# Lead of the query-row scores over the transposed scores in four-head attention tiles: two tiles before, one and a half after

## What is computed

```python
x = L0(x, ctx)      # causal self attention, cross attention, feed-forward; 16 heads of 16
x = L1(x, ctx)      # masked self and cross attention, 8 experts of which 2 per token; 16 heads of 16
x = L2(x, ctx)      # self and cross attention with masks and biases, feed-forward; 16 heads of 16
x = L3(x, ctx)      # causal cross attention, layer norm; 8 heads of 32

def attention(q, k, v, mask):          # per head
    s = q @ k.T * scale                # 512 x 512
    s = where(mask, -big, s)
    return softmax(s, axis=-1) @ v
```

## Time and profile before

| what | value |
| --- | --- |
| median of three executions | 2725.34 us |
| the profiled execution | 2719.28 us |
| its span | 2717.3 us |
| PE busy | 2500.1 us, 92% of the span |
| DVE busy | 1783.6 us, 66% |
| ACT busy | 1381.5 us, 51% |
| POOL busy | 739.8 us, 27% |
| mean granted clock of PE | 0.956 of 2.4 GHz |

### The profile page before, as it was taken

How to read it: one execution, slowest core, us unless ns; L and a number is a source line. 1 busy time by engine, 2 the same in 40 slices (tenths; PEclk the granted TensorE clock), 3 DMA queues, 4 the chain that set the end, 5 groups by cost and what they waited for, 6 DMA issues and landing times. The chain is left out here.

```text
span 2717.3 us, 44289 instructions
## 1 busy us (share of the span) xinstructions
PE 2500.1 (92%) x16014; PEld 1373.0 (51%) x16014; DVE 1783.6 (66%) x4364; ACT 1381.5 (51%) x1921; POOL 739.8 (27%) x867
## 2 busy tenths in 40 slices
PE   6999999988999999997999997799999999797896
PEld 3544433333444444443999997334434444385553
DVE  3566777777677777774457774577777777455554
ACT  1544455544555555555357875255555555452332
POOL 2243335433321110201016564102222112223012
PEclk7999999989999999998899999699999999998998
DMA  6222222122133223220127785422322322001331
GB/s 177 53 50 71 58 61 65 37 54 61 43 96 94 70 75 92 78 53 25 40 86 217 221 221 130 115 71 78 108 61 73 91 73 60 9 1 42 83 85 41
DMA packets 102212, 218.54 MB, mean 80 GB/s; under 512 B 19116, under 2 KB 35372, under 8 KB 100716
## 3 DMA queue, kind: packets, MB, share of 16 engines
q1 hardware_dynamic: 93164, 203.66, 27.5%
q0 software_dynamic: 8832, 12.06, 2.4%
HBM read 100.34 MB, written 12.58 MB: 42 GB/s over the span
## 5 line engine op out<-in xcount | busy, mean ns | idle before, releaser
L1120 ACT ACTIVATE probT_a<-scores 128x1024 f32<-128x1024 f32 (+3 forms) x832 | 779.0, 947 | 712.5 <-PE scores L951 420.6
L1228 DVE CUSTOM_DVE_ANT_0 ring<-ring,maskb_a 128x512 f32<-128x512 f32 x1024 | 686.3, 716 | 172.9 <-PE ring L969 163.6
L969 PE MATMUL ring<-stacks_a 64*128 64x512 f32 (+7 forms) x1664 | 468.2, 461 | 53.3 <-DVE negm_a L1226 17.3
L990 PE MATMUL outputs<-probT_a,V_a 128*32 128x512 f32 (+6 forms) x3328 | 443.9, 576 | 12.5 <-ACT oT_a L1129 8.5
L1226 DVE TENSOR_REDUCE negm_a<-ring 128x1 f32<-128x512 f32 (+3 forms) x640 | 332.1, 563 | 139.7 <-PE ring L975 105.4
L930 PE MATMUL scores<-stacks_a 64*128 64x512 f32 (+7 forms) x1664 | 399.7, 449 | 2.4 <-DMA stacks_a<-narrow_a 2.4
L969 PEld LDWEIGHTS ring<-stacks_a 64*128 64x128 f32 (+1 forms) x1664 | 211.7, 190 | 376.0 <-issue 140.2
L930 PEld LDWEIGHTS scores<-stacks_a 64*128 64x128 f32 (+1 forms) x1664 | 170.7, 187 | 249.6 <-issue 151.9
L889 POOL TENSOR_SCALAR maskb_a<-ints_a 128x1024 bf16<-128x1024 int32 x31 | 112.8, 3639 | 423.5 <-DMA ints_a<-in_mask 353.4
L899 POOL TENSOR_TENSOR ve<-mv,epsilon 128x1 f32<-128x1 f32 x96 | 18.2, 190 | 725.0 <-DVE mv L1195 725.0
L951 PE MATMUL scores<-maskT_a,identb 64*64 64x512 bf16 x1024 | 211.0, 402 | 0.0
(11 more groups left out here) (240 smaller groups left out, 3741.0 us busy)
## 6 DMA issues: line engine op xcount, KB each, us to landing
stacks_a<-parts_a SPq DMA_DIRECT2D x672, 128.0 KB
raw<-in_moew SPq DMA_DIRECT2D x92, 512.0 KB, 3.9
ints_a<-in_mask SPq DMA_DIRECT2D x31, 512.0 KB, 3.7
swapped_a<-maskT_a SPq DMA_DIRECT2D x32, 256.0 KB, 3.7
wt<-in_w SPq DMA_DIRECT2D x7, 1024.0 KB, 4.9
kvT_a<-in_ctxT SPq DMA_DIRECT2D x12, 512.0 KB, 3.4
wrow<-in_row SPq DMA_DIRECT2D x7, 512.0 KB, 5.9
stacks_a<-narrow_a SPq DMA_DIRECT2D x224, 8.0 KB
```

The lines of the kernel that those rows point to most:

```text
L969: last = pe.matmul(bank("S", j, n, e)[:, 0:w], Q[rows, g, qt * P:(qt + 1) * P], K[rows, g, 0:w], start=True, stop=not a.causal)
L990: last = pe.matmul(OB[x * slot:(x + 1) * slot, q0:S], V[:, m % 2, kb, c:c + slot], probT[:, kb % 2, x, q0:S], start=(kb == 0), stop=(kb == ...
L1120: act.activation(probT[:, kb % 2, 2 * p:2 * p + 2, q0:S], scores_bank(j, n)[:, :, q0:S], ACT.Exp, bias=0.0, scale=-1.0).then_inc(c_exp.sem, 1)
L1228: least = dve.tensor_tensor_reduce(sc, sc, maskb[:, m % 2, qt, :], 1.0, BIG * 2, ALU.add, ALU.min, out)
```

## The change

S of half h of the list no longer belongs to the tile two on. With 8 halves, the first four halves of tile j carry S of halves 4 to 7 of tile j+1, and the last four carry S of halves 0 to 3 of tile j+2. With 4 halves it is 2 and 2. S of tile j+1 thus ends with half 3 of tile j (half 1 in a6) and no longer with half 7 of tile j-1. split moves from half 0 to half 3 (1 in a6), m and mrows from half 2 to half 5 (from 1 to 2 in a6). Nothing else moves; no instruction is added or removed.

```diff
@@ timetable
     for u in range(QT):
         out += [(u * h + 1 + late, "oT", 0, u - 1), (u * h, "stack", 0, u + 3),
-                (u * h, "split", 0, u + 1), (u * h + step, "m", 0, u + 1),
-                (u * h + step, "mrows", 0, u + 1)]
+                (u * h + h // 2 - 1, "split", 0, u + 1), (u * h + h // 2 - 1 + step, "m", 0, u + 1),
+                (u * h + h // 2 - 1 + step, "mrows", 0, u + 1)]
@@ schedule
         for h in range(halves):
+            ahead, at = divmod(halves // 2 * 3 + h, halves)
             kinds = (("ST", "S", "exp") if not reorder else ("ST", "exp", "S") if h % couples else ("S", "ST", "exp"))
             for kind in kinds:
-                if kind == "S" and there(j + 2):
-                    yield (kind, j + 2, h)
+                if kind == "S" and there(j + ahead):
+                    yield (kind, j + ahead, at)
```

## The result

The changed kernel takes 2741.95 us (median of 8 runs, 2735.74 to 2750.48); the kernel before, on the same chip, 2724.89 (8 runs, 2718.28 to 2728.38). The ratio is 1.0065, 95% interval 1.0049 to 1.0081: **slower by some 17 us**, where 17 us faster were forecast. The profiled execution took 2742.99 us with a span of 2741.0; the one before had a span of 2717.3. The two profiles are thus 23.7 us apart, since the profiled execution of before lies 6 us under its median.

A forecast was written before the change was run, and what follows sets the result against it. The prediction took the masked stages, 64 of 112 tiles, as bound by PE's own work. Its terms, 4.9 + 6.4 + 1.1 + 4 + 2 - 1.4 = 17.0 us less, gave 2708 us, range 2694 to 2722.

The forecast's parts named there:

- the drain: End of a block, without S: shorter halves before mrows is needed, nothing to 1 us once per block; taken as nothing.
- a step that I had down at 1.4: In a6, m moving from half 1 to 2 loses 3.6 us cover, gives back half of 4.5: net -1.4.
- The two terms that were priced: In a6: lost cover for PE's waits before PV, 3.6 us; half of m's 4.5 us wait for DVE's norms regained.
- mrows comes late: Rival, chance 0.08: in a0 and a6 ST waits for mrows; at 1 us a tile 31 us more, 2739.
- First block: Start of a0: first V into PE's wait, m earlier, m to ST shorter; ST 8.2 us earlier, net gain 4.9.
- the third term: Start of a0: m to ST falls from 8.27 us to 4.5, with two halves of S left: 3.8 less.
- Second and third block: Starts of a4 and a6: second gains net 6.4 us (8.5 less 2.1 for returning S), third 1.1 (2.8 less 1.7).
- Masks: In a4 and a5, S comes four halves later against the mask, DVE's waits go: 4 us, between 2.5 and 5.3.
- Layer norm stretches: In a0, S's wide extremes no longer coincide with DVE's norms: 2 us gained, between 0 and 4.5.
- The clock comes back: Rival, chance 0.20: in a0 and a1 half the slow-clock loss behind the norms' waits ends; 15 us more gained, 2693.
- V stays where it counts: Rival, chance 0.18: at the starts V waits, or the second V costs what the first saves; 9 us go, 2717.
- It washes out: Rival, chance 0.09: the starts gain, a6 and the norms give it back; 2724.

The follow-up runs named there:

- m_only: Kernel before with only split, m and mrows moved to the later halves, S left where it was: 2758.76 us, ratio 1.0114.
- after_oT3: Changed kernel with ACT's copy oT one half earlier except in u = 1: 2718.66 us, ratio 0.9974.
- v_ahead: Kernel before with only the first V of each block's first unit put ahead of its first S: 2722.82 us, ratio 0.9993.
- one_half: Kernel before with S one half later in the list, split and m where they were: 2723.50 us, ratio 0.9992.
- after_oT: Changed kernel with ACT's copy oT one half earlier in every tile: 2746.15 us, ratio 1.0066.
- after_m4: Changed kernel with m and mrows one half earlier (half 4) where a tile has eight halves: 2744.27 us, ratio 1.0070.
- after_fill: Changed kernel with the projections of half 4 put into half 2 (half 1 in the third block), the place m left: 2745.15 us, ratio 1.0072.
- before_oT3: Kernel before with ACT's copy oT one half earlier except in u = 1: 2703.89 us, ratio 0.9919.

## Why the prediction was wrong

**The step that failed** is the first one: "the masked stages, 64 of 112 tiles, are bound by PE's own work. The change adds and removes no instruction there, so their pace stays". That PE is busy 75.84 of 76.50 us says that nothing is waited for in the order of before. It does not say by how little. m was costed at the cover it gives in a6 only, where the trace already showed a wait ahead of the V product; in the masked stages hardly any of that wait was in the trace because m stood in front of it. The rule that I had written for a6 (m's 0.6 us are part of the cover of oT) holds in the masked tiles with u = 1 and u = 3 too, at 0.50 us in the tile shown, and the new place had a price of its own, 0.37. Per unit of a2 and a3 that is 0.88 + 0.88 - 0.24 = 1.5 us (u = 2 takes 0.24 less), in a4 and a5 1.1 to 1.3; the tiles u = 1 to 3 of the 16 masked units took 20 us more, the masks' gain left out. Most of the rest was lost in a0, where m's move was named but not priced, and at the end of a6, where the drain was put at nothing. m_only shows the sum: 32 us for a step that I had down at 1.4, with the masks' gain already taken off.

**a6.** The two terms that were priced came out near: from a6's first exp on, PE's waits before the V products, for oT and for the exponentials, grew by 3.8 us (8.7 to 12.5; 3.6 forecast), and m's fell from 4.5 to 2.3 (half of it was forecast). But a6 took 12.6 us more, not 1.4, and 9.4 of these are at its end, where two tiles took 4.3 and 5.2 us more: the drain, which the prediction put at nothing. m_only has 4.2 and 4.1 there, so this too comes mostly with the move of split, m and mrows. after_oT3 gives 10.2 us of a6 back with the copy alone, but the kernel before gains 7.3 there by the same copy. Timeline, PE, kernel after:

```profile
2694.75 0.60 PE L1015 MATMUL ring<-identf,mx_a 128*32 128x128 f32 x4 [1.87 <-DVE mx_a L1238]
...
2700.55 1.22 PE L931 MATMUL scores<-stacks_a 128*128 128x512 f32 x2 [2.05 <-DMA stacks_a<-narrow_a]
```

m waits for split, the next ST for mrows, and then the granted clock is down for 17.1 us. Windows, kernel after and kernel before:

```profile
2696.40:2713.50 17.10, 13.57 (x54) 7.06 (x54) 3.41 (x8) 4.01 (x7) 0.73 (x1) 0.50 0.10 33
```

```profile
2680.00:2690.00 10.00, 8.96 (x59) 4.44 (x58) 2.34 (x6) 4.60 (x9) 1.70 (x3) 1.00 0.17 55
```

That is the rival "mrows comes late", with 11.1 us in 11 waits (2.4 in one before), 7.1 of them in eight of a6's tiles, where it had 31, and nearly none in a0's tiles (0.4). Which of the waits brings the clock down there was not tried.

**First block.** Timeline, PE, kernel after:

```profile
38.45 0.47 PE L970 MATMUL ring<-stacks_a 64*128 64x128 f32 x2 [7.46 <-DMA stacks_a<-swapped_a]
...
39.05 3.73 PE L1054 MATMUL ring<-wt,xT_a 128*128 128x256 f32 x8
...
55.04 1.06 PE L1015 MATMUL ring<-identf,mx_a 128*32 128x128 f32 x4
...
59.16 0.79 PE L931 MATMUL scores<-stacks_a 64*128 64x512 f32 x2 [0.90 <-DMA stacks_a<-narrow_a]
```

The first V (it stands in the second tile before the block, not the third) did go into the wait (11.16 us in the earlier trace rows, 7.46 now), and from m to ST it is 4.12 us, against 4.5 forecast. But m comes at 55.04, as before at 55.07: ST is 4.2 us earlier, not 8.2, and first S to ST takes 20.7 us, not 16.1. What failed is the step that V's 3.3 us and the half of S ahead of m (1.1) bring m forward: the work that was left ahead of m took as long as all of it had. Windows of that stretch, kernel after and kernel before:

```profile
43.50:53.00 9.50, 9.35 (x26) 4.45 (x25) 5.89 (x14) 0.00 (x0) 0.00 (x0) 0.50 0.28 64
```

```profile
43.90:53.00 9.10, 7.94 (x37) 4.40 (x36) 6.02 (x12) 1.20 (x2) 0.00 (x0) 1.00 0.33 77
```

Before, S ran at 2.4 GHz there; I had read the clock from 53 us on only. Now all of it and the second V (3.73 us, 1.95 before) run at 1.2 GHz. Going by the row was right for the third term: m to ST is 4.15 us shorter, 3.8 were forecast. The Trainium skill ("TensorE: Matmul & The Clock Gate", What's actually happening) has sustained work lift the clock. The trace after disagrees as that of before did: PE busy 9.35 of 9.5 us stayed at the low level.

**Second and third block.** The starts got shorter, and by more than forecast: first S to ST 18.8 us (1744.71 to 1763.51; 21.2 forecast), m to ST 4.14; the seam is 9.0 us shorter, where 8.5 was the sum before S's return. The halves of S that return cost less than I took: 0.9 us at the end of each of the two blocks (last tiles of a3 and a5 against m_only), not 2.1 to 3.3. Third block: 12.6 us from first S to ST (13.0 forecast), the seam 4.7 shorter (2.8). Which of the terms was larger than forecast is open; v_ahead has V's alone at 1.3 and 0.5 us.

**Masks.** DVE's wait for maskb is gone, and the size was near: tiles 74, 78 and 82, counted from 0 through all stages, fell by 2.46, 1.71 and 1.14 us, of which some 0.23 each is what every tile with u = 2 lost; 4.6 are left (4 forecast). The reason given, that S comes four halves later, is not the only one: m_only leaves S where it was, and they fell there by 2.45, 1.72 and 1.16. In the kernel before POOL waited for the second mask load (timeline, POOL):

```profile
1944.66 3.63 POOL L889 TENSOR_SCALAR maskb_a<-ints_a 128x1024 bf16<-128x1024 int32 x1 [5.86 <-DMA ints_a<-in_mask]
```

In m_only the same instruction:

```profile
1970.92 3.63 POOL L889 TENSOR_SCALAR maskb_a<-ints_a 128x1024 bf16<-128x1024 int32 x1 [3.51 <-DMA ints_a<-in_mask]
```

In three units of before POOL waited that long (5.9, 5.1 and 4.6 us); in m_only and in the changed kernel it waited 3.5 to 3.7 for every second load of a4 and a5 but that of the block's second unit, which runs in the start. In one_half it waited 4.59 once (at 2106.20), and DVE did not: there the later S hid it. Both ways work; which transfer had held up the load was not tried.

**Layer norm stretches.** S waits 2.2 us less for DVE in a0 (4.7 to 2.5 us, waits view), against 2 forecast, but m waits 6.3 there for the low parts (1.3 before), and a0 took 8.9 more, 5.9 of it PE busy longer.

**The other rivals.** "The clock comes back" did not come to pass: 0.94 in a0 (0.95 before), 0.97 in a1 (0.96). "V stays where it counts" was right for the first block, by its second half: the second V and S at the lower clock cost what the first V saved. At the other two v_ahead, with the first V alone ahead, brought 1.3 and 0.5 us, where 3.8 and 2.0 were forecast. "It washes out" fell short: a6 and the other tiles took back more than the starts gained.

## What to carry to other kernels

A stage in which an engine never idles is not proof that its order has slack: look at each wait of that engine that is zero in the trace, and ask which instruction stands in front of it and what is late the moment that one is moved. Before moving a small instruction in an order written out by hand, price both places: what it covered in the old one, and whose buffer it has to wait for in the new one. And when a moved piece costs more than it brings, the repair may be on another engine: a copy one half earlier on ACT was worth more (23 us) than all that the change had aimed at, in the kernel before as well as after.

## What the hardware showed that I had not expected

PE does the same work in a1 in all these kernels, but its busy time there went broadly with the mean granted clock: 271.6 us at 0.97 (changed kernel), 276.2 at 0.96 (before), 278.8 at 0.95 (after_oT), 284.4 at 0.92 (after_m4), 287.2 at 0.93 (after_fill), 285.6 at 0.91 (before_oT3). The clock in turn did not follow PE's idle time in a1: 42.6 us at 0.95 (after_oT), 37.9 at 0.97, 28.8 at 0.91. The stage's length is the sum of the two, from 307.5 to 323.5 us. Each is one profiled execution, but not chance alone: over the whole program the six executions of after_fill had 0.952 to 0.955, the eight of the changed kernel 0.957 to 0.964. What decides it is open; a change that is worth 10 us elsewhere can be lost in it.
